# A four-layer graph network: V's projection moved into the scatter loop, two edge comparisons for each K pass, and ten one-hot chunks made by GpSimd and ScalarE

## The reference

```python
bias = jnp.full((n, n), NEG); bias = bias.at[diag, diag].set(0.0)
bias = bias.at[dst, src].set(edge_weight)      # the last edge of a pair wins
q, k, v = jnp.split(x @ Wqkv.T + bqkv, 3, axis=-1)          # 8 heads of 64
scores = einsum('hnd,hmd->hnm', q, k) / 8 + bias
h = layer_norm(x + (softmax(scores) @ v) @ Wo.T + bo);  h = layer_norm(h + h @ W1.T + b1)
```

## Time and profile before

| what | us |
|---|---|
| three runs | 548.53, 551.04 (median), 551.95 |
| the profiled execution: its own time | 546.77 |
| its span, from first to last instruction | 544.7 |
| granted TensorE clock, mean | 0.963 of full |
| busy: PE, DVE, ACT, POOL | 471.8, 327.9, 161.0, 140.9 |

### The profile page before, as it was taken

How to read it: one execution, slowest core, us unless ns; L and a number is a source line. 1 busy time by engine, 2 the same in 40 slices (tenths; PEclk the granted TensorE clock), 3 DMA queues, 4 the chain that set the end, 5 groups by cost and what they waited for, 6 DMA issues and landing times.

```text
span 544.7 us, 6588 instructions
## 1 busy us (share of the span) xinstructions
PE 471.8 (87%) x2153; PEld 279.6 (51%) x2153; DVE 327.9 (60%) x577; ACT 161.0 (30%) x334; POOL 140.9 (26%) x151
## 2 busy tenths in 40 slices
PE   5789969767786799999899999866788799998995
PEld 2433327555555699944344444454564388443442
DVE  6987776787877997368812410159999810167114
ACT  1131134644544667311110102232242332002010
POOL 9300003434237700012200530045650620002000
PEclk9899997999888789999999999979999999999998
DMA  8800000000004100626240020000000400000002
GB/s 279 294 2 0 1 0 2 1 2 1 1 1 183 51 1 2 238 75 229 77 135 1 0 77 1 0 1 0 1 1 0 155 0 1 0 0 1 1 0 77
DMA packets 13599, 25.78 MB, mean 47 GB/s; under 512 B 896, under 2 KB 1280, under 8 KB 13568
## 3 DMA queue, kind: packets, MB, share of 16 engines
q1 hardware_dynamic: 13568, 25.38, 13.2%
HBM read 24.33 MB, written 1.05 MB: 47 GB/s over the span
## 4 chain that ended last, share of the span: by engine, by line
PE 59%; DVE 29%; issue 5%; ACT 3%; DVEq 2%; POOL 1%; ACTq 0%; POOLq 0%
PE ring L1130 31%; PE banks L1288 6%; PE ring L1136 4%; DVE G L1074 3%; DVE G L1091 3%; DVE G L1080 3%; PE ring L1207 3%; PE ring L1216 3%; DVE W_SD L832 3%; PE ring L1388 3%; PE banks L1388 3%; DVE W_SD L839 2%; DVE G L897 2%; PE banks L1244 2%; PE ring L1372 2%
## 5 line engine op out<-in xcount | busy, mean ns | idle before, releaser
L1130 PE MATMUL ring<-G,WA 128*128 128x512 f32 x160 | 70.2, 594 | 3.1 <-ACT WA L524 2.5
L439 POOL TENSOR_TENSOR A_SD<-A_SD,HH 128x128 f32 x64 | 34.1, 533 | 115.3 <-ACT HH L574 101.2
L463 POOL TENSOR_TENSOR RB<-X,vec 128x512 f32<-128x512 f32 x16 | 22.8, 1432 | 109.8 <-DVE X L971 108.4
L1130 PEld LDWEIGHTS ring<-G,WA 128*128 128x128 f32 x160 | 29.8, 190 | 38.4 <-issue 35.7
L1244 PE MATMUL banks<-RB,WB 128*128 128x128 f32 x256 | 46.0, 308 | 0.0
L975 DVE TENSOR_TENSOR HH<-ring,RB 128x512 f32<-128x512 f32 x14 | 9.6, 685 | 53.0 <-PE ring L1130 53.0
L1074 DVE TENSOR_REDUCE G<-ring 128x256 f32<-128x2048 f32 x8 | 18.3, 2292 | 36.6 <-PE ring L1372 36.4
L1244 PEld LDWEIGHTS banks<-RB,WB 128*128 128x128 f32 x256 | 37.9, 210 | 0.0
L806 DVE TENSOR_REDUCE HH<-banks 128x6 f32<-128x768 f32 x32 | 30.5, 957 | 10.5 <-PE banks L1200 10.5
L524 ACT ACTIVATE WA<-ring 128x512 f32<-128x512 f32 x42 | 24.1, 590 | 40.7 <-PE ring L1136 40.6
L538 ACT ACTIVATE sd<-mv,eps 128x1 f32<-128x1 f32 x32 | 9.4, 294 | 86.9 <-DVE mv L951 86.9
(11 more groups left out here) (183 smaller groups left out, 875.9 us busy)
## 6 DMA issues: line engine op xcount, KB each, us to landing
WA<-in_wqkv SPq DMA_DIRECT2D x2, 1024.0 KB, 8.1
WC<-in_w SPq DMA_DIRECT2D x2, 1024.0 KB, 8.4
WB<-in_wo SPq DMA_DIRECT2D x2, 1024.0 KB, 6.3
G<-in_w SPq DMA_DIRECT2D x1, 2048.0 KB, 10.7
G<-in_w SPq DMA_DIRECT2D x2, 1024.0 KB, 6.7
WA<-in_xT SPq DMA_DIRECT2D x4, 256.0 KB, 4.1
WA<-in_wqkv SPq DMA_DIRECT2D x4, 256.0 KB, 4.3
vec<-in_g SPq DMA_DIRECT2D x4, 256.0 KB, 8.2
```

Of the source, the lines that this page charges most:

```text
L439: pool.tensor_tensor(win, win, cnt_g[:, q, :, :], ALU.add).then_inc(group_added, 1)
L463: pool.tensor_tensor(out_, x_, vec[:, slot[vector], :], ALU.add).then_inc(resid_ready, 1)
L1130: last = nc.tensor.matmul(t[:, :], lhs(k), rhs_(k), start=(k == 0), stop=(k == n_k - 1))
```

## The change

- V's 16 passes leave the comparison part. Each K pass is followed by two comparisons instead of one; V's pass c is done at the end of chunk c of the scatter loop, in a ring bank that it holds for four chunks (`ring_banks`). ScalarE copies V's block b out after chunk 4b+3.
- The score products of chunk c are done three chunks ahead (`AHEAD`), behind the second group of a chunk; those of chunks 0 to 2 stand before the loop. ScalarE widens one chunk ahead, behind the second group's counts, and no longer two.
- Early one-hots are now 12 chunks: 0 and 1 by VectorE as before, 2 to 11 by GpSimd (iota minus key, L477) and then ScalarE in place (square, L594; relu(1 - d*d), L596). Chunks 8 to 11 lie in `WC`, whose load of w10 moves behind x and wo0. VectorE makes `src_hot` in the loop for chunks 12 to 15 only.
- VectorE's `dst_hot` of chunks 0 and 1 move from behind the comparisons to in front of them.
- In the loop VectorE's sequencer computes the next window's start right behind a `clear`, and a 1 x 1 copy (`touched`) uses it there, so that it is computed there; the next chunk's word is loaded behind the fourth clear.
- In the code part, TensorE turns the edge numbers before the tile ranges, GpSimd's fills wait for VectorE (`edges_float`, `code_ready`), and VectorE's base chain is woven between the copies of codes.

```diff
-EARLY = NI // 2
+EARLY = 3 * NI // 4
+AHEAD = 3
@@ gpsimd
+            pool.wait_ge(edges_float, 2)
             pool.memset(ones_row[:, :], 1.0).then_inc(consts, 1)
...
+            pool.wait_ge(code_ready, 2)
             pool.memset(A_SD[:, :, :], 0.0).then_inc(zeroed, 1)
...
+            pool.wait_ge(early_ready, 2)
+            for c in range(2, EARLY):
+                pool.tensor_tensor(src_hot_of(c), iota_2[...], lo_key[...], ALU.subtract).then_inc(key_distance, 1)
@@ scalar
-            for b in range(NB):
-                evac(("KT", b), KB[:, b, :], bias=col[:, 1, b:b + 1])
-            for b in range(NB):
-                evac(("V", b), VB[:, b, :])
+            def early_hots(c):
+                act.wait_ge(key_distance, c - 1)
+                act.activation(src_hot_of(c), src_hot_of(c), ACT.Square).then_inc(distance_squared, 1)
+                act.wait_ge(distance_squared, c - 1)
+                act.activation(src_hot_of(c), src_hot_of(c), ACT.Relu, bias=1.0, scale=-1.0).then_inc(early_ready, 1)
+            for c in range(2, EARLY):
+                early_hots(c)
+                if c % 3 == 1:
+                    evac(("KT", c // 3 - 1), KB[:, c // 3 - 1, :], bias=col[:, 1, c // 3 - 1:c // 3])
+            evac(("KT", NB - 1), KB[:, NB - 1, :], bias=col[:, 1, NB - 1:NB])
...
+            for c in range(AHEAD):
+                for name in beside_scatter()[c]:
+                    take_beside(name)
...
-                for c in range(2):
-                    widen(c, src_hot_of(c), src_hot_at(c), None)
+                widen(0, src_hot_of(0), src_hot_at(0), None)
                 for c in range(NI):
-                    take_beside(c)
                     for q in range(GI):
                         take_counts(c * GI + q, q)
-                    if c + 2 < NI:
-                        widen(c % 2, src_hot_of(c + 2), src_hot_at(c + 2), (c + 1) * GI)
+                        if q == 1 and c + 1 < NI:
+                            widen((c + 1) % 2, src_hot_of(c + 1), src_hot_at(c + 1), c * GI or None)
+                        if 1 <= q <= 2 and c + AHEAD < NI:
+                            take_beside(beside_scatter()[c + AHEAD][q - 1])
+                    take_value(c)
@@ vector
-            for c in range(4, EARLY):
+            for c in range(2):
                 early_hots(c)
+            for c in range(2):
+                dst_hots(c, chunk(column_key, c))
             for p in range(PAIRS):
...
+                word = word_of(0)
+                base = window_start(word, 0)
                 for c in range(NI):
-                    word = dve.value_load(packed_i[0:1, c:c + 1], min_val=0, max_val=(1 << 28) - 1)
                     g, more = c * GI, c + 2 < NI
                     for q in range(GI):
-                        win = clear(g + q, q, window_start(word, q))
+                        win = clear(g + q, q, base)
+                        if q == GI - 1 and c + 1 < NI:
+                            word = word_of(c + 1)
+                        if q < GI - 1 or c + 1 < NI:
+                            base = window_start(word, (q + 1) % GI)
+                            dve.tensor_copy(touched[:, g + q:g + q + 1], zero_row[:, bass.ds(base, 1)])
@@ tensor
-            pe.wait_ge(dst_relative, 1)
...
-                    compare(b * NB + k)
+                    for p in range(2):
+                        compare((b * NB + k) * 2 + p)
             pe.wait_ge(loads["wv0"], 16)
-            for b in range(NB):
-                t = claim(("V", b))
-                for k in range(NB):
-                    last = nc.tensor.matmul(t[:, :], cols(XT, k, b), WA[:, 2, k, :], start=(k == 0), stop=(k == NB - 1))
-                    ...
-                    compare((NB + b) * NB + k)
...
+            for c in range(AHEAD):
+                beside(c)
...
                 for c in range(NI):
-                    beside(c)
...
                     for q in range(GI):
                         group(c * GI + q, q, c % 2, src_hot_of(c))
+                        if q == 1 and c + AHEAD < NI:
+                            beside(c + AHEAD)
+                    value_pass(c)
```

More of the change, by code:

```diff
@@ L60, in ring_order @@
         add("KT", (b,), "A")
-    for b in range(NB):
-        add("V", (b,), "A")
-    for names in beside_scatter():
+    for c, names in enumerate(beside_scatter()):
         for name in names:
             add(name[0], name[1:], "A")
+        for b in range(NB):
+            if c == min(b * NB + NB - 1 + AHEAD, NI - 1):
+                add("V", (b,), "A")
     for b in range(NB):
@@ L127, with ring_banks @@
     EMPTIED[_name] = (_engine, 1 + sum(e == _engine for _, e in ORDER[:_k]))
+def ring_banks():
+    claims = [name for name, _ in ORDER]
+    for b in range(NB):
+        claims.remove(("V", b))
+        claims.insert(claims.index(beside_scatter()[b * NB + AHEAD][0]), ("V", b))
+    bank_at, before, last_in, turn, held = {}, {}, {}, 0, None
+    for name in claims:
+        if name[0] == "S":
+            turn += turn % R == held
+        elif name[0] != "V":
+            turn = POS[name]
+        bank_at[name] = turn % R
+        held = turn % R if name[0] == "V" else held if name[0] == "S" else None
+        before[name] = last_in.get(turn % R)
+        last_in[turn % R] = name
+        turn += 1
+    return bank_at, before
+RING_BANK, RING_BEFORE = ring_banks()
 VECTORS_0 = ["bv0", "bo0", "b10", "g10", "be10", "g20", "be20"]
@@ L177, in gnn_program @@
         eps = sb("eps", [P, 1])
+        zero_row = sb("zero_row", [1, N], BF16)
+        touched = sb("touched", [1, NG], BF16)
         st = sb("st", [P, STAT_SLOTS, 8])
@@ L324, in bank_of @@
         def bank_of(name):
-            return ring[POS[name] % R]
+            return ring[RING_BANK[name]]
         def src_hot_at(c):
@@ L361, in _ @@
             load("bv0", vec[:, slot["bv0"], :], a["bqkv0"][2 * D:3 * D].partition_broadcast(P))
-            load("w10", WC[:, :, :], blocks(a["w10"]))
             for v in VECTORS_0[1:] + ["bias1", "b3"]:
@@ L368, in _ @@
             load("wo0", WB[:, :, :], blocks(a["wo0"]))
+            load("w10", WC[:, :, :], blocks(a["w10"]))
             wait_full(sp, ("BD", NB - 1))
@@ L754, in early_hots, with take_codes @@
                 hot(src_hot_of(c), chunk(lo_key, c)).then_inc(early_ready, 1)
-            for r in range(4):
+            def take_codes(r):
                 dve.wait_ge(codes_turned, 2 * r + 1)
                 dve.tensor_copy(rows_l[:, r * 1024:(r + 1) * 1024], turned_codes[0]).then_inc(rows_l_ready, 1)
-                early_hots(r)
             dve.wait_ge(ranges_turned, 1)
@@ L1143, in _ @@
             pe.wait_ge(consts, 1)
+            pe.wait_ge(edges_float, 2)
+            pe.wait_ge(loads["ew"], 16)
+            for k in range(3):
+                last = nc.tensor.transpose(bank[2][:, k * P:(k + 1) * P], nat[:, k, :], ident[:, :])
+            last.then_inc(edges_turned, 1)
             pe.wait_ge(tile_ranges, 2)
@@ L1148, in _ @@
             last.then_inc(ranges_turned, 1)
-            pe.wait_ge(loads["ew"], 16)
-            for k in range(3):
-                last = nc.tensor.transpose(bank[2][:, k * P:(k + 1) * P], nat[:, k, :], ident[:, :])
-            last.then_inc(edges_turned, 1)
             def turn_codes():
```

78 lines of the change are left out of this document (51 added, 27 removed).

## The result

| | us |
|---|---|
| before, 4 runs | 551.01 (548.53 to 551.95) |
| changed, 4 runs | 536.36 (534.42 to 537.77) |
| ratio, 95% interval | 0.974 (0.969 to 0.978) |
| forecast | 546.3 (537 to 554) |
| profiled execution of the changed kernel: time, span | 536.35, 534.6 |

What follows compares the result with a forecast made beforehand. TensorE was taken to bound the comparisons, VectorE and its register work the scatter loop. Terms +0.5 - 11.9 - 0.9 + 7.6 = -4.7 us, from a median of 551.04 to 546.3 us, range 537 to 554.

Steps and rivals of the forecast that it cites:

- item 2: Scatter loop: the word's load and register work ahead of weight_hot start it at about 1.0 us, not 0.20: +0.8 us.
- item 1: Scatter loop: register work between fold and clear gets shorter, a gain of 0.2 us a chunk.
- Up to the first reduction: Before the comparisons: second dst hot meets GpSimd's first difference, +0.5 us; code part edits taken as nothing.
- Comparison part: Comparisons: VectorE becomes the bound at 0.90 us for each of 32 reductions, -11.9 us with GpSimd and ScalarE hidden.
- rival B: Early hots: GpSimd's differences are late and delay ScalarE and the loop; about 560 us, chance 0.14 counting TensorE's lower clock.
- To the first clear: Last reduction to first clear: dst hots gone, ScalarE's six copies and widening a little shorter than VectorE's way, -0.9 us.
- The loop: Scatter loop as a whole: register work, load and first chunk against four src hots fewer, +7.6 us.
- Item 4: Scatter loop, chunks 8 to 11: four src hots fewer at 0.48 us each, -1.9 us.
- Item 5: Scatter loop: TensorE has room for V's pass except at the lower clock in the first chunk, +1.5 us.
- A: Scatter loop: register work is hidden, a chunk costs 0, first chunk loses nothing; 536 to 539 us, chance 0.28.
- C: Scatter loop: sequencer doesn't run ahead, `touched` waits for the clear, +0.6 us a chunk more; about 554 us, chance 0.13.
- sign of being wrong: Scatter loop: the prediction called itself wrong if a chunk in the middle took under 5.2 us.

Runs made afterwards that it cites:

- e3: The changed kernel with GpSimd's first difference waiting for both dst hots, not only for the two early src hots: 533.54 us, ratio 0.971.
- e10: e9 plus eight fp32 matmuls that nobody reads, put in TensorE's idle time among the first comparisons: 527.43 us, ratio 0.961.
- e9: e7 with ScalarE widening chunk 0 ahead of its six copies of scores: 527.23 us, ratio 0.962.
- e6: The kernel before with only the loop's new register code (and the row of zeros `touched` copies from): 551.36 us, ratio 1.004.
- e4: The changed kernel with VectorE making all twelve early hots ahead of the comparisons, GpSimd's and ScalarE's part gone: 540.00 us, ratio 0.983.
- e8: The kernel before with GpSimd's addition of counts cut to 16 of the window's 128 columns, counts incomplete: one profiled run of 547.35 us.
- e5: The changed kernel with twelve of V's sixteen passes left out, V incomplete: 535.95 us, ratio 0.975.
- e2: The changed kernel with the word's load, its window start and `touched` moved from in front of weight_hot to behind it: 532.50 us, ratio 0.968.
- e1: The changed kernel with the old register code in the loop, without the `touched` copy: 538.49 us, ratio 0.979.
- e7: The changed kernel with the edits of e2 and e3 together: 531.49 us, ratio 0.966.

## Why the prediction was wrong

Up to the last clear the terms of the forecast add up to -4.7 us, and the traces have -12.7. One step failed, item 2 of the loop, and it is worth 7.7 of the 8.0 us together with item 1. The other 2 us of the measured 14.65 lie in which execution was profiled and in the clock behind the loop.

- **Up to the first reduction (+0.5, measured +0.06).** The second dst hot met GpSimd's first difference, as said, but dearer: the pair took 2.98 us, and 1.29 without the meeting (e3), 1.69 in all. The earlier trace rows showed such a hold and was read as a bound of 1.1. The rule of the Trainium skill that was weighed there ("SBUF — State Buffer", section "SBUF: two separate sides") is an exclusive lock for a whole instruction. This trace agrees: the difference runs from 33.77 to 36.04 us, and the hot, shown from 34.20 on, ends only at 36.58. It made the sum 1.2 us worse and not the forecast 1.8, since the difference had begun 0.4 us before the hot. The total is right by luck: the edits of the code part, taken as nothing, brought the hots forward by 1.6 us (32.39 for 34.03). VectorE was ready earlier still. Its cast started at 5.80 us and not 8.65 and took 3.26 for 4.65, and it then waited 4.15 us for TensorE's spread bases (31.47). Which of these edits did it was not tried.
- **Comparison part (-11.9, measured 30.62 for 40.98, -10.36).** The mechanism held: 0.90 us for each reduction once it ran. What was left out are the 1.94 us of waits at its start: TensorE, idle while VectorE makes hots, comes back at the 1.2 GHz level, and e10, with the idle time filled, has no such wait. GpSimd and ScalarE were done when forecast, so rival B fell.
- **To the first clear (-0.9, measured -0.46).** The path was named (six copies, then the widening) and its length taken as a little shorter than VectorE's; it was 2.7 us longer. e9 took this out.
- **The loop (+7.6, measured -1.9).** Here the prediction failed, in item 2: "In the new order that operation is dst_hot, so the load starts about 0.13 us after the clear's start." The load starts 0.29 us *before* the clear (92.76 and 93.05).

  The rule read from 15 loads was counted wrongly. In the old order the operations ahead of the load are the clear (just ended), weight_hot (running) and the fold (still queued): one runs, one is queued. (The load ahead of the loop, at 80.69, which the prediction took for an exception, is the same case: dst_hot just ended, one weight_hot running, one queued.) In the new order the two are dst_hot and the fourth clear, so the count does not hold the load once the fold before them has ended. What the load then waits for is the clear's own wait for that fold, which stands ahead of it in the sequencer's order, and one register row: it starts 0.23 us after the fold's end in all of the loop's 15 loads, beneath dst_hot in 14 and with no dst_hot there in the last. So it does in e6 (fold's end at 107.92, load at 108.15), and in one load of e4, where the clear also waited for ScalarE's counts, it came 0.62 us after the fold.

  So weight_hot starts at 0.59 us or less in 13 of 14 chunks (0.93 in one) and not at 1.0: mostly +0.38 or less, not +0.8. Item 1 gained 0.38 a chunk and not 0.2 (0.16 us in each of two windows and 0.06 at the first). Together nothing (e6: +0.26 us over the whole loop) in place of +8.0.
- **The rest of the loop.** Item 4 held: a src hot costs 5.64 - 5.03 = 0.61 us a chunk after and 5.45 - 5.05 = 0.40 in e8, so four of them 1.6 to 2.4 us (forecast 1.9). Item 5: the first chunk cost 0.87 us more (forecast 1.5), by its clock: in e3 and e5, at 1.00, it took 1.25 us less and so was shorter than before's. And one term was missing: in before, weight_hot was held off by GpSimd in six chunks, 14 of them 17.8 us together, and in the changed kernel in three (17.2 us). That is 0.6 us, and it is most of the 5.26 to 5.03 of a middle chunk. e6 still has the hold, so it isn't the register code that ended it; which edit did was not tried.
- **Behind the last clear** the profiled pair gave 2.6 us back. Before's execution had a granted clock of 1.00 over 434 to 445 us, the changed one 0.84 over the like stretch (422 to 433 us), and e8 alone of the experiments is like before there. That does not settle it: this part takes 378.4 us in e8 at the full clock and 377.7 in e9 with the lower one. What sets the clock there was not tried.
- **The rivals.** A had the time and, by its numbers, the mechanism: +0.4 us for the load, 0.3 gained by item 1, a chunk that costs 0 (measured +0.38, 0.38 and 0). It was wrong on its name, since the register work is not hidden (e2: 0.25 us a chunk where it stands), and on a first chunk that loses nothing. Part of its fit in the total is luck, by the 4.3 us under which before was profiled. The sign of being wrong that the prediction set for itself, a middle chunk under 5.2 us, came true (5.03). B's sum was off: 17 us on 546.3 are 563 and not 560. Its argument that GpSimd's additions take the same whatever stands beside them does not hold either: in before the 128x512 addition (L463) takes 1.26 to 1.77 us. C, a sequencer that does not run ahead, fell with the 0.82 us windows.

## What to carry to other kernels

Before costing a run-time value or a load on an engine's instruction stream, list the operations ahead of it in the old and in the new order and count how many are still pending when it starts. List too what those operations wait for, since a load stands behind their waits. Then it costs what sticks out behind them, and behind a long operation it cost nothing that these runs show. When two engines share a resource for a whole instruction, or one is left idle for two microseconds ahead of a bound part, look there first for what a plan lost: the order of a load, a wait and a widening (e9) took back 9.3 us up to the last clear, beyond the change. And take a full row of matmuls as a question: leave some out and see.

## What the runs showed of the hardware

- A VectorE operation on SBUF that is issued while a GpSimd addition runs ends later by the time until that one ends, less 0.12 us: 1.42 us for 1.20 where the addition ended 0.34 us in (before, 104.03), 1.45 where it ended 0.38 us in (after, 119.48), 1.28 at 0.19 (e1, 105.21), nothing at 0.11 (e8). An addition of GpSimd that met weight_hot took 0.96 us for 0.45 (before, 104.80). The reductions from PSUM beside ten GpSimd differences kept their 0.96 us (after).
- A GpSimd difference of 128x1024 in bf16 with repeated rows takes 1.89 us in its row, 1.86 from start to start (after, from 38.30), and 2.27 and 2.33 beside VectorE's dst hots; the fp32 addition of that size takes 2.34.
- VectorE's sequencer starts a 0.30 us load with one operation running and another queued, 0.05 us after the operation before these has ended (before, all 16 loads, of which the last has none queued; e2, the 14 behind a hot). Behind a clear that waits for a fold it starts 0.23 us after the fold's end, and 0.22 us of the load and of its register rows then stuck out (after, idle time before `touched`, 88.52).
- The same 2.2 us of idle time of TensorE ahead of the loop were followed by the lower clock in four profiles (after, e1, e4, e7) and not in three (e2, e3, e5). Idle stretches of 1.98 us and more among the first comparisons were followed by it in all eight. Where the idle time was shortened to 0.27 us (e9, ahead of the loop) or filled up to 0.64 (e10, among the comparisons), one profile each, the clock stayed at 1.00.
